# Two token groups of the last layer turned in its first supersteps, with a router for each pair of groups

## The reference, cut to what matters

```
x = hidden_states                                     # layer-normalised residual
router_probs = softmax(x @ w_router)
gate_weights = softmax((x @ w_gating) / 0.1)
g = einsum('bsh,ehf->ebsf', x, w_gate)                # 8 experts, F = 1024
u = einsum('bsh,ehf->ebsf', x, w_up)
expert_out = einsum('ebsf,efh->ebsh', silu(g) * u, w_down)
cw = router_probs * gate_weights
cw = cw / (sum(cw, -1) + 1e-9)
out = einsum('ebsh,bse->bsh', expert_out, cw)         # added to the residual
```

## Time and profile before

| | us |
|---|---|
| median of 3 runs | 1722.78 |
| lowest and highest | 1720.77, 1730.06 |
| the profiled execution, its own time | 1729.01 |
| its span from first to last instruction | 1727.2 |
| PE busy in the span | 1592.0 (92%) |
| DVE, ACT, POOL busy | 1207.6, 874.6, 661.6 |
| mean granted PE clock | 0.958 |

### The profile page before, as it was taken

How to read it: one execution, slowest core, us unless ns; L and a number is a source line. 1 busy time by engine, 2 the same in 40 slices (tenths; PEclk the granted TensorE clock), 3 DMA queues, 4 the chain that set the end, 5 groups by cost and what they waited for, 6 DMA issues and landing times. The chain is left out here.

```text
span 1727.2 us, 25997 instructions
## 1 busy us (share of the span) xinstructions
PE 1592.0 (92%) x7985; PEld 1289.0 (75%) x7986; DVE 1207.6 (70%) x2226; ACT 874.6 (51%) x1548; POOL 661.6 (38%) x585
## 2 busy tenths in 40 slices
PE   6998997779984888889999999999999999999998
PEld 5796673368882777768888888778788788788787
DVE  6656677736665789567677777767766776876875
ACT  4455332134432456555665665665655655656653
POOL 2542156688806634330540530521612603604500
PEclk9998898889995999889999999999999999999999
DMA  6994022168843212000100100101101101001001
GB/s 201 271 326 196 4 71 100 58 209 258 255 137 114 80 37 74 1 1 27 55 31 31 58 10 31 67 0 49 49 0 49 49 9 57 32 12 55 31 13 50
DMA packets 74493, 136.38 MB, mean 79 GB/s; under 512 B 8592, under 2 KB 52176, under 8 KB 74256
## 3 DMA queue, kind: packets, MB, share of 16 engines
q1 hardware_dynamic: 40544, 92.76, 16.4%
q10 hardware_dynamic: 27696, 25.51, 4.7%
q0 software_dynamic: 6144, 16.79, 3.1%
HBM read 90.93 MB, written 44.11 MB: 78 GB/s over the span
## 5 line engine op out<-in xcount | busy, mean ns | idle before, releaser
L1355 DVE TENSOR_TENSOR gU<-ps,gU 128x512 f32<-128x512 f32 x384 | 257.7, 686 | 78.3 <-PE ps L2565 67.3
L1348 DVE TENSOR_TENSOR eL<-eF,eH 128x512 fp32r<-128x512 f32 x256 | 191.9, 750 | 161.7 <-ACT eH L1828 161.7
L2041 POOL TENSOR_TENSOR cL<-cR,cH 128x384 fp32r<-128x384 f32 x192 | 211.8, 1129 | 241.5 <-ACT cH L1733 241.5
L1812 ACT ACTIVATE gU<-ps 128x512 f32<-128x512 f32 x384 | 225.7, 597 | 128.1 <-PE ps L2565 112.0
L1828 ACT ACTIVATE eH<-eF 128x512 fp32r<-128x512 f32 x256 | 161.2, 630 | 162.6 <-DVE eF L1343 162.1
L2565 PE MATMUL ps<-xTH,cH 128*128 128x512 f32 x512 | 204.2, 399 | 10.2 <-DVE eF L1343 5.9
L2565 PE MATMUL ps<-xTH,cL 128*128 128x512 f32 x512 | 202.1, 395 | 0.0
L2565 PE MATMUL ps<-xTL,cH 128*128 128x512 f32 x512 | 201.9, 394 | 0.0
L2585 PE MATMUL ps<-eH,cL 128*128 128x512 f32 x480 | 189.1, 394 | 0.0
L2585 PE MATMUL ps<-eH,cH 128*128 128x512 f32 x480 | 188.4, 393 | 0.0
L2028 POOL TENSOR_TENSOR cR<-cR 128x256 f32<-128x256 f32 x32 | 34.1, 1065 | 397.0 <-DMA cR<-in_w 397.0
(11 more groups left out here) (439 smaller groups left out, 3454.1 us busy)
## 6 DMA issues: line engine op xcount, KB each, us to landing
cR<-in_w SPq DMA_DIRECT2D x32, 768.0 KB, 4.1
slots_in<-eS SPq DMA_DIRECT2D x16, 768.0 KB, 10.4
eS<-in_wr SPq DMA_DIRECT2D x32, 384.0 KB, 4.3
xl<-slots_in ACTq DMA_DIRECT2D x48, 256.0 KB, 3.9
slots_out<-yo ACTq DMA_DIRECT2D x48, 256.0 KB, 3.2
cwB<-expert_weights SPq DMA_DIRECT2D x16, 512.0 KB, 3.4
k_parts<-parts SPq DMA_DIRECT2D x8, 512.0 KB, 5.5
q_parts<-parts SPq DMA_DIRECT2D x8, 512.0 KB, 3.9
```

The costliest lines, as they stand in the source:

```text
L1348: dve.tensor_tensor(eL[:, b, :], eF[:, b, :], f32(eH[:, b, :]), ALU.subtract).then_inc(block_low, 1)
L1355: dve.tensor_tensor(to[:, :], ps[:, 2 + half, :], to[:, :], ALU.add).then_inc(half_summed, 1)
L1812: act.activation(to[:, :], ps[:, half, :], ACT.Identity).then_inc(snap_done, 1)
L2041: last = pool.tensor_tensor(cL[c][:, cols_], cR[c][:, cols_], f32(cH[c][:, cols_]), ALU.subtract)
```

## The change

Seven edits that go together:

- PE: block B3 has no turn and no router any more. Group L2 is turned in superstep 0 after P1 (into banks 4 and 5), and the logits of pair 0 are computed in superstep 0 after P7 (bank 6). Group L3 is turned in superstep 1 after unit 0. The logits of pair 1 are computed in superstep 5. The weights are turned once for each pair, in supersteps 2 and 6.
- PE waits for `pair_ready` of pair 1 only at superstep 4.
- ACT: `normalise("L", 2)` comes after the last silu of B3 and after `residual_added` 4, `turned("L", 2)` in superstep 0. `exponentials(p)` is done for each pair, in supersteps 1 and 5, ahead of `gate` 2. `sums_of(1)` moves from superstep 1 to 2.
- DVE: in B3 `spread("L", 2)` stands after `ffn_low` 1 and `roots("L", 2)` after `ffn_low` 2. `last_even(2)` is in superstep 0. `spread` and `roots` of L3 come later in superstep 0. The six parts of `last_odd(3)` are spread over supersteps 1, 2 and 3. `router_shift` of pair 0 is in superstep 0 and of pair 1 in superstep 5, `router_weights(p)` in supersteps 1 and 5.
- SP stores and broadcasts the weights for each pair; the second store stands ahead of the loads of expert 1's chunks.
- `cwc` is laid out by pair, and `rt0` lies elsewhere.
- Sizes of all matmuls and transfers stay, but for the store of the weights in two halves.

```diff
-                rows = cw_d.rearrange("(e n) p -> e (n p)", n=NT)[:, p * 1024:(p + 1) * 1024]
+                rows = cw_d[64 * p:64 * p + 64].rearrange("(e n) p -> e (n p)", n=8)
...
-            sp.wait_ge(turned_copied, 5)
-            sp.dma_start(cw_d, cwT[:, :]).then_inc(cw_stored, 16)
-            sp.wait_ge(cw_stored, 16)
-            load_weights_of(0, 0)
-            sp.wait_ge(mix_read, 4)
-            load_weights_of(0, 1)
+            for p in range(2):
+                sp.wait_ge(turned_copied, 5 + p)
+                sp.dma_start(cw_d[64 * p:64 * p + 64], cwT[0:64, :]).then_inc(cw_stored, 16)
+                sp.wait_ge(cw_stored, 16 * p + 16)
+                wait(sp, mix_read, 4 * p)
+                load_weights_of(0, p)
...
             ffn_low("B", 3, 0)
             block_out("B", 2)
+            ffn_low("B", 3, 1)
             spread("L", 2)
+            ffn_low("B", 3, 2)
             roots("L", 2)
-            ffn_low("B", 3, 1)
-            ffn_low("B", 3, 2)
-            last_even(2)
             ffn_low("B", 3, 3)
-            router_shift(5, 0, 8, 1)
             block_out("B", 3)
...
                 if start:
-                    spread("L", 3)
+                    last_even(2, 4)
                 if first and s == 1:
                     last_odd(3, 0, 6)
-                    last_odd(3, 1, 6)
-                    last_odd(3, 2, 6)
-                if first and s == 2:
+                if first and s == 5:
                     router_shift(2, 8, 8, 2)
                 half_sum(e, s, 0, 0)
                 half_sum(e, s, 0, 1)
                 if start:
-                    roots("L", 3)
+                    spread("L", 3)
+                if first and s == 1:
+                    last_odd(3, 1, 6)
                 hidden(e, s, 0)
                 hidden_rest(e, s, 0)
-                if first and s == 1:
-                    last_odd(3, 3)
                 half_sum(e, s, 1, 0)
                 half_sum(e, s, 1, 1)
+                if start:
+                    roots("L", 3)
                 hidden(e, s, 1)
                 if s % 4 == 0:
                     mixed(e, s, 0, 0)
                 hidden_rest(e, s, 1)
-                if first and s == 1:
-                    last_odd(3, 4)
-                    last_odd(3, 5)
+                if start:
+                    router_shift(6, 0, 8, 1)
                 hidden(e, s, 2)
                 half_sum(e, s, 2, 0)
                 half_sum(e, s, 2, 1)
                 hidden_rest(e, s, 2)
                 if s % 4 == 0:
                     mixed(e, s, 1, 0)
+                if first and s == 1:
+                    router_weights(0)
+                    last_odd(3, 2)
                 if first and s == 2:
-                    router_weights()
+                    last_odd(3, 3)
+                    last_odd(3, 4)
+                if first and s == 3:
+                    last_odd(3, 5)
+                if first and s == 5:
+                    router_weights(1)
...
             ffn_silu("B", 3, 0)
-            normalise("L", 2)
             ffn_silu("B", 3, 1)
             for part in range(3):
                 high(0, 1, part)
             ffn_silu("B", 3, 2)
-            turned("L", 2)
             ffn_silu("B", 3, 3)
             act.wait_ge(residual_added, 4)
+            normalise("L", 2)
...
                 snapshot(e, s, 0, 1)
+                if start:
+                    turned("L", 2, bank=4)
...
-                if first and s == 3:
-                    act.wait_ge(turned_done, 5)
-                    act.activation(cwT[:, :], ps[:, 2, 0:P], ACT.Copy).then_inc(turned_copied, 1)
+                if first and s in (2, 6):
+                    p = s // 4
+                    act.wait_ge(turned_done, 5 + p)
+                    wait(act, cw_stored, 16 * p)
+                    act.activation(cwT[0:64, :], ps[0:64, 2, 0:P], ACT.Copy).then_inc(turned_copied, 1)
...
                 if start:
                     normalise("L", 3)
-                if first and s == 1:
-                    sums_of(1)
                 gate(e, s, 1)
                 high_of(e, s, 1)
+                if first and s in (1, 5):
+                    exponentials(s // 4)
+                if first and s == 2:
+                    sums_of(1)
                 gate(e, s, 2)
                 high_of(e, s, 2)
-                if first and s == 2:
-                    exponentials()
...
-            block("B", 3, {3: ("L", 2)}, 5)
+            block("B", 3, {})
...
+                if first and s % 4 == 0:
+                    pe.wait_ge(pair_ready, s // 4 + 1)
                 both("P1")
+                if start:
+                    pe.wait_ge(evac_done, 4 * (M_L1 - 1))
+                    turn("L", 2, bank=4)
+                if first and s == 1:
+                    pe.wait_ge(xT_low, 8 + 2 * TURNS.index(("L", 3)))
+                units(0)
                 if first and s == 1:
                     pe.wait_ge(logits_read, 1)
-                units(0)
-                if first and s == 2:
+                    turn("L", 3, bank=6)
+                if first and s == 5:
                     pe.wait_ge(half_summed, 6 * s)
                     router_logits(2, 1)
-                if first and s == 3:
+                if first and s in (2, 6):
+                    p = s // 4
                     pe.wait_ge(half_summed, 6 * s)
-                    pe.wait_ge(cw_done, 1)
-                    pe.transpose(ps[:, 2, 0:P], cwc[:, :, :].rearrange("p e n -> p (e n)"), ident[:, :]).then_inc(turned_done, 1)
+                    pe.wait_ge(cw_done, p + 1)
+                    pe.transpose(ps[0:64, 2, 0:P], cwc[:, p, :, :].rearrange("p e n -> p (e n)"), ident[:, :]).then_inc(turned_done, 1)
...
                 both("P2")
                 both("P7")
+                if start:
+                    pe.wait_ge(evac_done, 4 * M_L1)
+                    router_logits(6, 0)
...
                 units(3)
-                if start:
-                    pe.wait_ge(evac_done, 4 * M_L1)
-                    turn("L", 3, bank=6)
```

More of the change, by code:

```diff
@@ L97, in build @@
         cw2 = at("cw2", [P, NT, 16])
-        cwc = at("cwc", [P, E1, NT], F32, start["cw2"])
+        cwc = at("cwc", [P, 2, E1, 8], F32, start["cw2"])
         st = at("st", [P, NT, 6])
@@ L265, in build @@
         tm = at("tm", [P, 2, 512], F32, start["mx8"])
-        rt0 = at("rt0", [P, NT, 16], F32, start["mx8"])
+        rt0 = at("rt0", [P, NT, 16], F32, start["wk"])
         rt1 = at("rt1", [P, NT, 8], F32, end["rt0"])
-        assert end["tm"] <= start["idS"]
+        assert end["tm"] <= start["wk"] and end["rt1"] <= start["zcol"]
         ps = ctx.enter_context(nc.psum_tensor("ps", [P, 8, 512], F32))
@@ L1115, in turned_low, with last_even @@
                                       ALU.subtract).then_inc(xT_low, 1)
-            def last_even(g):
+            def last_even(g, bank=2):
                 for c in range(2):
                     dve.wait_ge(xT_copied, copies("L", g) + c + 1)
-                    dve.tensor_copy(xTF[:, c, g * 512:(g + 1) * 512], ps[:, 2 + c, :]).then_inc(xT_low, 1)
+                    dve.tensor_copy(xTF[:, c, g * 512:(g + 1) * 512], ps[:, bank + c, :]).then_inc(xT_low, 1)
             def last_odd(g, part, bank=2):
@@ L1199, in router_shift, with router_weights @@
                 dve.tensor_scalar(s1v[:, :, 1, :], s1v[:, :, 1, :], 10.0, None, ALU.mult).then_inc(shifted_done, 1)
[L1201 to L1212, removed]
+            def router_weights(p):
+                r = slice(8 * p, 8 * p + 8)
+                s1v = rt0[:, r, :].rearrange("p n (a e) -> p n a e", a=2)
+                dve.wait_ge(exp_done, 2 + p)
+                link(dve.tensor_reduce(sm[:, r, :], s1v, AXX, ALU.add))
+                link(dve.reciprocal(sm[:, r, :], sm[:, r, :]))
+                link(dve.tensor_tensor(s1v, s1v, sm[:, r, :].unsqueeze(3).to_broadcast([P, 8, 2, E1]), ALU.mult))
+                link(dve.tensor_tensor(rt1[:, r, :], s1v[:, :, 0, :], s1v[:, :, 1, :], ALU.mult))
+                link(dve.tensor_reduce(sm2[:, r], rt1[:, r, :], AXX, ALU.add))
+                link(dve.tensor_scalar(sm2[:, r], sm2[:, r], 1e-9, None, ALU.add))
+                link(dve.reciprocal(sm2[:, r], sm2[:, r]))
+                dve.tensor_tensor(cwc[:, p, :, :].rearrange("p e n -> p n e"), rt1[:, r, :], sm2[:, r].unsqueeze(2).to_broadcast([P, 8, E1]),
                                   ALU.mult).then_inc(cw_done, 1)
@@ L1455, in _ @@
                     acc = ps[:, 4 + 2 * j + t // 2, (t % 2) * D:(t % 2) * D + D]
-                    dve.scalar_tensor_tensor(x[:, tile, :], acc, cwc[:, E1 - 1, tile:tile + 1], x[:, tile, :], ALU.mult, ALU.add).then_inc(out_ready, 1)
+                    dve.scalar_tensor_tensor(x[:, tile, :], acc, cwc[:, 1, E1 - 1, tile - 8:tile - 7], x[:, tile, :], ALU.mult, ALU.add).then_inc(out_ready, 1)
         @block.scalar
@@ L1723, in _, with exponentials @@
                 weight_high("B", i)
```

(19 more changed lines are left out.)

## The result

| | median us (runs) | ratio to before, 95% interval |
|---|---|---|
| before | 1724.79 (22) | |
| changed | 1732.02 (22) | 1.0042 (1.0031 to 1.0052) |

A forecast was written before the change was run, and what follows sets the result against it. Only the 107.8 us before superstep 4 were taken to have loss, 30 us in waits and low clock; PE bounds the rest. Terms -8.0 + 3.4 + 7.2 - 8.6 + 2.8 + 10.5 = +7.3, taken as +6.5: 1729 us, range 1718 to 1739.

The forecast's parts named there:

- the likeliest case: Whole kernel: slower by 0 to 8.6 us, within half a per cent; chance 0.47.
- block B3: Block B3: turn and router leave, ScalarE stands until 694.0; PE ends down 3 at 705.5 against 713.5, -8.0 us.
- superstep 0: Superstep 0: turn of L2, router of pair 0 and low clock come in; 16.6 us against 13.2, +3.4.
- door and superstep 1: Start and whole of superstep 1: late hidden(2), turn of L3, gate(2) wait; 24.6 us against 17.4, +7.2.
- superstep 2: Superstep 2: router 1 and last_odd pieces leave its front, waits for weights and cwT remain; 20.5 us against 29.1, -8.6.
- superstep 3 and door of 4: Superstep 3: 0.5 us at P7, 2.4 before P1 of superstep 4, 1.0 for clock, against 1.1 before; +2.8.
- supersteps 5 and 6 (with 4): Supersteps 5 and 6: router of pair 1 with low clock, 4.45 + 2.75, waits 0.4 and 2.1, clock 0.8; +10.5 us.
- ScalarE held by POOL's sums: Block B3: ScalarE reaches high(0, 1) at 687.6 and stands until POOL's last sum ends at 694.0.
- the chain: Superstep 1's start: half_sum, roots, normalise, gate, hidden, high_of, hidden_rest, router_shift, hidden(2) one after another, 9.5 us; PE starts at 728.6, not 722.8.
- Table loads: Around exponentials, before gate(2): four loads instead of two, 1.28 us each, without the skill page's drain of 1380 ns.
- the rival of the spreading clock: New waits in superstep 2 and before 4 and 6 cost 3.4 us each: +7.4 more, 1737 us; within slower outcomes, 0.36.
- The weights' queue: SP: load_chunk(1, 0) now also behind superstep 6's cwT, store and broadcast; cost taken as 0, at worst 2 us.

The follow-up runs named there:

- the high part last: Changed kernel with ScalarE's three parts of chunk 1's high part behind the last silu of block B3 instead of between silus 1 and 2; ratio 1.0009 to the kernel before.
- the kernel with the later shift: Changed kernel with router_shift of pair 0 behind hidden(2) instead of ahead of it; one execution, stretch from B3 to expert 1 173.3 us, no ratio.

## Why the prediction was right

The forecast of +6.5 us (sum +7.3) met a measured ratio of 1.0042, some 7.2 us, and it was a small loss inside half a per cent, the likeliest case. Term by term, in the profiled executions:

| term | forecast | measured |
|---|---|---|
| block B3 | -8.0 | -5.7 |
| superstep 0 | +3.4 | +4.7 |
| door and superstep 1 | +7.2 | +7.2 |
| superstep 2 | -8.6 | -9.4 |
| superstep 3 and door of 4 | +2.8 | +1.4 |
| supersteps 5 and 6 (with 4) | +10.5 | +10.3 |
| sum | +7.3 | +8.5 |

The main waits that it named all came, each at its place, and luck had a part in how close the sum came. Its misses have both signs (+2.3, +1.3, 0.0, -0.8, -1.4, -0.2). And the largest term, supersteps 5 and 6, holds a toll of the low clock behind the router that came out 1.6 us smaller in five other kernels with the same instructions there, and 3.2 smaller in one (see the last section).

**ScalarE held by POOL's sums** was right to 0.1 us at its end and is shown by the edit that took it away. The 0.1 is partly luck: I took POOL's times over unchanged, but chunk_rest(0, 0) began 0.7 us ahead of B3 (675.85) where it had begun 0.7 behind its start, and took 9.24 us instead of 8.37, and the sums took 0.5 longer; the two cancelled. The sign that I had named, a wait of some 6 us ahead of ffn_down(3, 2), came as 3.3 us: PE ran dry 13.3 us after the start of B3 and not 10.5, since it had waited 2.2 us for its first low part and lost some more at the low clock behind that. This did not move the end of the block, which hung on ScalarE and VectorE.

The B3 term was mis-sized at its next step: "I take 4.0 (ends 1.9 and 4.1)" for roots(L, 2) beside chunk_rest. They took 6.0, outside both ends:

```profile
693.00 0.97 DVE L1090 TENSOR_SCALAR vA<-mv 128x4 f32<-128x4 f32 x1
694.00 0.93 DVE L1099 TENSOR_SCALAR scl<-vA 128x4 int32<-128x4 int32 x1
694.97 0.91 DVE L1100 TENSOR_TENSOR u<-scl 128x4 f32<-128x4 f32 x1
...
698.40 0.57 DVE L1107 SCALAR_TENSOR_TENSOR ofs<-mv,scl 128x4 f32<-128x4 f32 x1
```

POOL meanwhile:

```profile
689.63 6.23 POOL L2050 TENSOR_TENSOR cL<-cR,cH 128x384 fp32r<-128x384 f32 x6 [0.96 <-ACT cH L1739]
695.82 0.72 POOL L2037 TENSOR_TENSOR cR<-cR 128x256 f32<-128x256 f32 x1
```

My upper bound was of another piece: 4.07 us beside POOL's sums, instructions of 0.73 us, while chunk_rest consists of instructions of 1.0 us (6.23 for six). With the high part last, the roots stood beside the sums and took 3.7 us. While chunk_rest ran, three operations took over 0.9 us; from 695.8 on POOL was back at sums and the operations behind the first of them alternate between 0.16 and 0.57, as in the earlier trace rows. The Trainium skill (SBUF — State Buffer, Who interferes with whom) calls the port pair that VectorE and GpSimd share an exclusive lock: the one that issues first has it, and the other waits. The trace agrees with that: the price goes by the length of POOL's instruction. The same section counts `tensor_scalar` among the operations that can enter the 2-port modes, and so contend with GpSimd. The trace agrees here too: `TENSOR_SCALAR` at 693.00, with one input of 4 elements, took 0.97 us. In all the last low part was there 1.8 us later than forecast, counted from the start of B3. The other 0.5 us of the 2.3 is the last ffn_down, 2.7 us at the low clock (699.75 to 702.48) where the sum had 2.2.

**Superstep 0** came out 1.3 us above the forecast because it began at that low clock: the granted clock was 0.51 from 694.5 to 704.9, so the first 2.3 us of the superstep ran at half the pace, an estimate of 1.2 us.

**The door of superstep 1** was right in size (4.9 us of wait, 24.5 us in all), and each of three links of the chain was taken out: the roots (and with them the normalising), the shift, and the clock behind it.

**Table loads** are as in the earlier trace rows: 1.28 us each, four instead of two, and the exponential starts at 744.50, 0.01 us behind the load. No drain of the size that the Trainium skill gives for a switch (ScalarE: Activation LUTs, What ACT_TABLE_LOAD costs) shows.

**Clock.** The terms that I gave to the low clock in supersteps 2 and 3 (1.0, 1.0) were too large: the clock was 1.00 in both. So the rival of the spreading clock fell for this kernel: behind the waits of 2.0 and 1.6 us close together around superstep 2 and the one of 1.7 at the door of 4 the clock stayed up. Behind the wait of 2.2 us in B3 it did not (0.61 from 683.3 to 687.7), nor behind those of 3.3 and 4.8 there or that of 3.7 at the door. The length of the wait does not settle it: the wait of 2.0 us at the door of superstep 2 stands in seven of the kernels, and in five of them the low clock followed. In the kernel with the later shift, P1 of superstep 2 ran at 1.2 GHz behind it (first row below), six matmuls in 2.56 us. Superstep 2 took 18.0 us in all seven, since PE waits for the weights next: 1.6 us where the clock had stayed up, 0.4 or nothing where it had fallen.

```profile
743.65 0.63 PE L2571 MATMUL ps<-xTH,cH 128*128 128x512 f32 x1 [2.01 <-ACT eF L1824]
744.07 0.63 PE L2571 MATMUL ps<-xTH,cL 128*128 128x512 f32 x1
...
745.78 0.63 PE L2571 MATMUL ps<-xTL,cH 128*128 128x512 f32 x1
746.21 0.63 PE L2591 MATMUL ps<-eH,cH 128*128 128x512 f32 x1
```

In superstep 2 the single terms missed by more than their sum: the door took 2.0 us (forecast 1.1), the weights 1.6 (2.0), cwT 0.2 (0.9) and the clock nothing (1.0).

**The weights' queue** had slack. Between the sums of chunk (1, 0) and its chunk_rest, which needs ScalarE's high part in between, POOL stood idle for 3.4 us, against 10.5 before. ScalarE took the sums up 2.5 us after they were done:

```profile
842.07 2.00 POOL L2050 TENSOR_TENSOR cL<-cR,cH 128x384 fp32r<-128x384 f32 x2 [3.44 <-ACT cH L1739]
```

Why, then, does moving 7 us of idle and a router out of B3 gain nothing? Nowhere did the kernel get the removed idle time back whole, since something else was due next. In B3 ScalarE's fixed order put POOL's sums in line. The router and the turn need the same PE time elsewhere. And roots and normalising of L3, which had been hidden, came to lie behind the moved router.

## What to carry to other kernels

Before work is moved out of a block to remove a wait, walk each other engine's own list to the point where the wait ended: the next instruction that it holds may be due at almost the same time. Put an instruction that waits for a slow producer (here high(0, 1)) behind those that the busiest engine needs, and small chains (roots) where their engine stands idle anyway, not behind the longest wait of the superstep. A wait removed in one place can be several us dearer in the next, as the roots of L2 were behind the last low part: measure both ends.

## What the runs showed of the hardware that was not expected

The toll of the low clock behind the same instructions is not the same in every kernel. Superstep 5 of seven kernels has equal instructions (router of pair 1 and exponentials ahead of gate 2), and took 20.2 us in one, 21.8 in five and 23.4 in the changed kernel: steps of 1.6 us. By the granted clock behind the router, that is no piece at 1.2 GHz in the first, a short one in the five and one of twice the length in the changed kernel. Each is one execution of another kernel, so whether two executions of one kernel differ as much is not shown. The edits ahead of it are all over 50 us away, and nothing in them says why it should be longer. A gain under some 2 us in one profile can't be claimed from the sum of a stretch. It can from a wait that goes, but only where no low clock has taken that wait's place: the wait for the weights in superstep 2 was 1.6 us or nothing with equal instructions.
